# A decoder layer on one core: the order of its first phase rewritten, with 64-row self scores and both normalisations on ScalarE

## The chip, the cores and the metric

One core of a Trainium2 chip runs the whole kernel in one launch. The metric is the device time of an execution in microseconds (us); lower is better.

## What is computed

A transformer decoder layer (post-norm) over x of shape (32, 64, 256) with a context of the same shape:

```
h = LN(x + selfattn(x))              # 16 heads of 16, causal over 64 positions
h = LN(h + crossattn(h, ctx))        # 8 heads of 8 over the 256 channels as positions, rotary, softmax over 256
y = LN(h + ffn(h))                   # 256 -> 1024 -> 256, both matmuls with quantised weights and activations
def selfattn(x):  att = softmax(mask(q @ k.T / 4)); return (att @ v) @ w_out.T
def crossattn:    scores = rot(Wq x + bq) . rot(Wk c + bk) / sqrt(8); out = softmax(scores) @ (Wv c + bv); Wo out + bo
def ffn:          silu, gelu, LN, quantised linear layers
```

The self-attention has sequences of 64; the cross-attention treats the 64 positions of a sequence as channels and the 256 channels as its positions. Outer residuals and norms are those of the kernel's own stages (norm1, norm2, and the last norm in phase 3).

## The kernel before

The 32 sequences are taken as 16 pairs of 2 x 64 = 128 rows. Three phases follow each other, with a barrier between: the attention phase (the one that is changed), then two feed-forward phases, which take no part in the change but for norm2 of the last pair.

**Work of a pair in the attention phase.** Self-attention: qk_proj and v_proj (TensorE, fp32), qk_copy and v_copy (ScalarE), k_mask (GpSimd; the keys of a head are cut out by a mask so that one matmul gives several heads), scores (TensorE: a bf16 mask matmul, then fp32 scores on top in the same bank), minus_max (VectorE, row maxima, then the difference into SP), self_exp (ScalarE), self_sum (VectorE), self_norm (GpSimd), transpose_p, pt_copy, self_pv, ao_copy, out_proj. Then norm1_stats (VectorE), rstd (GpSimd), norm1 (VectorE, into X1), x_keep (ScalarE, X1 into XALL), rotary_proj q, rotate q (VectorE), split_parts q (GpSimd, three bf16 parts of an fp32 value), and over HBM into the expanded tile QA (store_parts, expand_rows). The context goes the same way to KA (rotary_proj k, rotate k, split_parts k). Cross-attention: sixteen tiles of max matmuls (mx_b) with a VectorE row maximum each; the maxima are negated in two bf16 parts (negate), transposed by TensorE (max_transpose), copied (mt_copy) and sent by two DMAs into rows 48 and 49 of QA (max_rows); sixteen tiles of exp matmuls (e_b) with ScalarE's exp into PB; eight pv_quad (P.V into u_b); u_copy, u_transpose, u_norm, att_transpose, at_copy, x_out_proj, norm2_stats, rstd, norm2 (VectorE), square_sum (ScalarE).

**Order.** It is written out by hand. Body i has sixteen steps S0 to S15, and all engines walk through them. In each step TensorE computes one max tile, 14 tiles ahead of the exp tiles (AHEAD), and one exp tile of pair i, two heads each, interleaved; every second step has a pv_quad. The other operations are put at fixed steps. A max tile needs the reduction of the tile two before it, an exp tile the exp of the one two before it. Everything else shares two PSUM banks, g_b[0] and g_b[1]: `use` makes TensorE wait, before it writes a bank, until the last reader of the group that was written there before is done, in the order of the program. So the order of the steps sets the waits.

Before, pair i+3 has its qk_proj at S0, v_proj at S11 and scores at S13 and S14 of body i, and its softmax, transposes, self_pv, out_proj, norm1 and q projection in S0 to S9 of body i+1. A prologue ahead of body 0 does three pairs by hand in three sets of banks (head_banks, tail_banks).

**Lines.** L443 qk_proj, L451 v_proj, L458 and L462 scores, L474 transpose_p, L487 self_pv, L496 out_proj, L508 and L509 rotary_proj, L516 xv_proj, L531 max tiles, L545 max_transpose, L559 exp tiles, L574 pv_quad, L230 u_transpose, L237 att_transpose, L242 x_out_proj; ScalarE L684 qk_copy, L702 self_exp, L709 pt_copy, L723 mt_copy, L729 exp_tile; GpSimd L818 k_mask, L823 self_norm, L831 to L841 split_parts; VectorE L850 and L854 minus_max, L862 and L864 self_sum, L869 to L873 norm1_stats, L880 norm1, L888 rotate, L278 to L283 norm2_stats, L287 norm2, L897 xv_bias, L907 max tiles, L918 and L920 negate.

## Time and profile before

| | |
|---|---|
| runs shown | 670.93 us median of 3 (668.68 to 674.22) |
| the profiled execution | 677.3 us, span 675.4 us from the first to the last instruction |
| TensorE, VectorE busy | 490.2 us (73%), 522.3 us (77%) |
| ScalarE, GpSimd busy | 378.3 us (56%), 319.9 us (47%) |
| mean granted clock of TensorE | 0.829 of full |
| DMA | 37.04 MB, mean 55 GB/s |

The attention phase takes the first 494 us of the span, the two feed-forward phases the rest. "Granted clock" is what the throttle leaves of TensorE's 2.4 GHz: 1.00 or 0.50. A stage is named by body: body i begins with the first exp tile of pair i.

### The profile page before, as it was taken

Reading aid. Unit: us, or ns where it says so; the run is one execution under the profiler, and the core shown is the slowest. Engines: PE = TensorE matmul, PEld = TensorE weight load, DVE = VectorE, ACT = ScalarE, POOL = GpSimd, SP = SyncE. Lnnn points to the kernel's source line nnn. Section 1 sums busy time; section 2 is a strip of 40 time slices with the busy share of each in tenths; the row PEclk is TensorE's granted clock in tenths of the full one; section 3 lists DMA queues with packets and bytes.
Section 4 is the critical chain, followed back from the end, with each engine's and each line's share of the span. In section 5 each row is a group of like instructions: output and inputs, shape, how many; then the busy total and the mean of one; then the engine's idle time right before and its main releaser. Section 6 shows DMA issues by size and latency. Waiting matters only on the chain. (4 is left out here: it accounts for less than half of the span.)

```text
span 675.4 us, 12183 instructions
## 1 busy us (share of the span) xinstructions
PE 490.2 (73%) x3986; PEld 253.3 (38%) x4002; DVE 522.3 (77%) x1045; ACT 378.3 (56%) x681; POOL 319.9 (47%) x383
## 2 busy tenths in 40 slices
PE   5556888889888888898898888788966414545445
PEld 3332435444444344444443444333222103333333
DVE  6476678978988879889888898778437677888885
ACT  1211346555556555555565656477548958677673
POOL 6442435364464553644645537320020057776773
PEclk9787779999999999999999999878567955555555
DMA  7212522212222223132222221220000000000000
GB/s 260 59 43 74 177 67 65 68 51 74 75 65 62 64 68 83 49 76 69 72 60 66 66 77 49 51 71 4 1 0 1 0 0 8 16 16 23 16 17 32
DMA packets 51400, 37.04 MB, mean 55 GB/s; under 512 B 21392, under 2 KB 47376, under 8 KB 51216
## 3 DMA queue, kind: packets, MB, share of 16 engines
q1 hardware_dynamic: 51344, 36.33, 18.8%
q8 instruction: 31, 0.51, 0.3%
q14 instruction: 25, 0.20, 0.1%
HBM read 24.52 MB, written 10.49 MB: 52 GB/s over the span
## 5 line engine op out<-in xcount | busy, mean ns | idle before, releaser
L729 ACT ACTIVATE PB<-e_b 128x512 f32<-128x512 f32 x256 | 149.5, 594 | 115.7 <-PE e_b L559 115.3
L907 DVE TENSOR_REDUCE MX<-mx_b 128x2 f32<-128x512 f32 x256 | 171.4, 681 | 44.0 <-PE mx_b L531 43.2
L531 PE MATMUL mx_b<-KA,QA 48*128 48x256 bf16 x512 | 101.3, 287 | 15.0 <-DMA QA<-parts_q 8.4
L559 PE MATMUL e_b<-QA,KA 50*128 50x256 bf16 x512 | 99.5, 289 | 9.6 <-DMA QA<-MR 7.4
L574 PE MATMUL u_b<-PB,VA 128*32 128x256 f32 x1024 | 88.7, 420 | 4.2 <-ACT PB L729 4.1
L823 POOL TENSOR_TENSOR SP<-SP,srec 128x1024 f32<-128x1024 f32 x14 | 26.6, 1901 | 101.4 <-DVE srec L864 101.4
L531 PEld LDWEIGHTS mx_b<-KA,QA 48*128 48x128 bf16 x512 | 31.5, 96 | 96.3 <-DVE MX L907 41.9
L1325 PE MATMUL r_b<-att_tab,Q 128*128 128x128 f32 x128 | 31.5, 427 | 37.5 <-ACT Q L1249 37.4
L818 POOL TENSOR_TENSOR KM<-QK,att_tab 128x1024 f32<-128x1024 f32 x30 | 57.0, 1904 | 1.6 <-ACT QK L684 1.6
L1317 PE MATMUL z_b<-w2q,Q2T 128*128 128x256 bf16 x128 | 30.2, 417 | 37.0 <-ACT Q2T L1272 26.3
L295 POOL TENSOR_TENSOR rs<-mv,epsc 128x1 f32<-128x1 f32 x32 | 6.1, 190 | 96.2 <-DVE mv L283 66.6
L1282 POOL TENSOR_TENSOR rsh<-mvh,epsc 128x1 f32<-128x1 f32 x16 | 15.2, 949 | 56.9 <-DVE mvh L1345 56.9
L1325 PEld LDWEIGHTS r_b<-att_tab,Q 128*128 128x128 f32 x128 | 25.1, 223 | 45.2 <-ACT Q L1249 38.1
L1292 POOL TENSOR_TENSOR N<-N,row_tab 128x1024 f32<-128x1024 f32 x16 | 37.6, 2349 | 1.9 <-ACT N L1256 1.9
L559 PEld LDWEIGHTS e_b<-QA,KA 50*128 50x128 bf16 x512 | 30.0, 96 | 20.1 <-DMA QA<-MR 11.1
L574 PEld LDWEIGHTS u_b<-PB,VA 128*32 128x32 f32 x1024 | 21.2, 112 | 40.4 <-ACT PB L729 25.6
L443 PE MATMUL g_b<-XT,wp 128*128 128x128 f32 x224 | 32.1, 303 | 5.7 <-DMA XT<-in_xT 5.7
L1317 PEld LDWEIGHTS z_b<-w2q,Q2T 128*128 128x128 bf16 x128 | 16.6, 141 | 49.3 <-DVE stz L1363 24.9
L443 PEld LDWEIGHTS g_b<-XT,wp 128*128 128x128 f32 x224 | 29.3, 211 | 11.0 <-DMA wp<-in_wpT 5.7
L462 PE MATMUL g_b<-KM,QK 128*64 128x512 f32 x112 | 30.2, 618 | 3.3 <-issue 3.3
L880 DVE TENSOR_SCALAR X<-Y,mv,rs 128x256 f32<-128x256 f32 x16 | 27.3, 1707 | 5.4 <-POOL rs L297 5.4
L831 POOL TENSOR_TENSOR full_k<-rot_k 128x256 f32<-128x256 f32 x16 | 11.6, 726 | 39.6 <-DVE rot_k L888 39.6
(197 smaller groups left out, 1125.4 us busy)
## 6 DMA issues: line engine op xcount, KB each, us to landing
KA<-parts_k SPq DMA_DIRECT2D x64, 96.0 KB
QA<-parts_q SPq DMA_DIRECT2D x64, 96.0 KB
parts_q<-part_q SPq DMA_DIRECT2D x32, 128.0 KB, 1.9
parts_k<-part_k SPq DMA_DIRECT2D x16, 192.0 KB, 2.1
XT<-in_xT SPq DMA_DIRECT2D x16, 128.0 KB, 2.4
X<-in_x SPq DMA_DIRECT2D x16, 128.0 KB, 2.2
C<-in_ctx SPq DMA_DIRECT2D x16, 128.0 KB, 2.1
out_y<-O SPq DMA_DIRECT2D x16, 128.0 KB, 1.7
```

Of the source, the lines that this page charges most:

```text
L443: last = nc.tensor.matmul(ps[:, P * c:P * c + P], wp[:, k, P * c:P * c + P], XT[:, a.p, k, :], start=k == 0, stop=k == 1)
L462: last = nc.tensor.matmul(ps[SEQ * b:SEQ * b + SEQ, :], QK[:, c, SEQ * b:SEQ * b + SEQ], KM[:, c, :, SEQ * b:SEQ * b + SEQ], start=False, ...
L531: m = nc.tensor.matmul(mx_b[n % 2][:, D * k:D * k + D], QA[low:low + K_MAX, 2 * i.ring + b, h, P * u:P * u + P], KA[low:low + K_MAX, 2 * i ...
L559: m = nc.tensor.matmul(e_b[n % 2][:, D * k:D * k + D], KA[low:low + K_EXP, 2 * i.ring + b, h, P * sc:P * sc + P], QA[low:low + K_EXP, 2 * ...
L574: last = nc.tensor.matmul(u_b[b][32 * j:32 * j + 32, D * s4:D * s4 + D], VA[:, i.p, sc, b, 4 * s4 + j, :], PB[:, (2 * m + j % 2) % 4, j // ...
L729: nc.scalar.activation(PB[:, n % 4].rearrange("p e t -> p (e t)"), e_b[n % 2][:, :], ACT.Exp, scale=XC ** -0.5).then_inc(e_sb.sem, 1)
L818: ops.tensor_tensor(KM[:, c], QK[:, 2 + c, :].unsqueeze(1).broadcast_to([P, 8, P]), kmask.unsqueeze(2).broadcast_to([P, 8, P]), ALU.mult). ...
L880: nc.vector.tensor_scalar(X1[:], Y1[:], mv1[:, 0:1], rs1[:, 1:2], ALU.subtract, ALU.mult).then_inc(ln1.sem, 1)
L907: nc.vector.tensor_reduce(MX[:, b, e, 2 * q:2 * q + 2, u], mx_b[n % 2][:, :].rearrange("p (e s) -> p e s", e=2), AXL.X, ALU.max).then_inc( ...
L1292: nc.gpsimd.tensor_tensor(N[:, k.p, :], N[:, k.p, :], gam, ALU.mult).then_inc(zg.sem, 1)
L1317: m = nc.tensor.matmul(z_b[j.p][:, 0:D], Q2T[:, j.p, k, :], w2q[:, k, :], start=k == 0, stop=k == 7)
L1325: t = nc.tensor.transpose(r_b[j.p][:, P * k:P * k + P], Q2[:, j.p, P * k:P * k + P], ident)
```

## The change

Only the attention phase is changed (and norm2 of the last pair). 

- Order: the whole self-attention of pair i+3 up to self_pv lies in body i (qk_proj S1, scores S5, transpose_p S13, self_pv S14); out_proj, norm1 and the q projection follow in S0 to S3 of body i+1. The prologue is gone: the bodies run from -4 (LEAD) and leave out what isn't there yet. All of it uses g_b[0] and g_b[1].
- Scores: k_mask makes 4 heads per chunk instead of 8; after two mask matmuls there are eight score matmuls of 64 rows, 64 columns and 256 moving columns, row half r into bank g_b[r], with one signal at the end. The row maximum and the difference go bank by bank, at S5 to S8; the exp is in two halves.
- Maxima of the cross-attention: MX (fp32) goes through TensorE as an fp32 matmul against the identity; mt_copy writes the negated high part (bf16) and mt_low (VectorE) the low part, instead of the two negations ahead of the transposition. The two DMAs of max_rows carry high and low rows instead of the two halves.
- norm1 and norm2 are applied by ScalarE (scale and bias), straight into XALL; rstd (GpSimd) gets a third operation for the bias. norm2_max stays on VectorE.
- The bias of the cross values is added after the softmax, in at_copy; xv_bias (VectorE) becomes xv_copy (ScalarE).
- Start: the fill of KA moves from GpSimd to VectorE, the small fills, VM and VA to GpSimd; the context has four buffers; row_tab is loaded later. TensorE waits for the two casts before its first matmul.
- SP's order per body: expand k, max_rows(i,1), store and expand q, loads, max_rows(i+1,0), store k, cross_values.

```diff
-            def scores(a, chunks=(0, 1)):
-                for c in chunks:
-                    ps = use(head_banks(a)[1 - c], sc_sub, a, 2 * c + 2)
+            def scores(a):
+                for r in range(2):
+                    ps = use(g_b[r], sc_sub, a, 2 * r + 2)
                     nc.tensor.matmul(ps[:, :], identb[:], maskb[:].rearrange("p h s -> p (h s)"),
                                      start=True, stop=False, skip_group_check=True)
+                for c in range(2):
                     wait(pe, km, a, c + 1)
-                    for b in range(2):
-                        last = nc.tensor.matmul(ps[SEQ * b:SEQ * b + SEQ, :], QK[:, c, SEQ * b:SEQ * b + SEQ],
-                                                KM[:, c, :, SEQ * b:SEQ * b + SEQ],
-                                                start=False, stop=True, skip_group_check=True)
-                    last.then_inc(sc_ps.sem, 1)
+                    for r in range(2):
+                        for b in range(2):
+                            last = nc.tensor.matmul(g_b[r][SEQ * b:SEQ * b + SEQ, D * c:D * c + D],
+                                                    QK[HALF * r:HALF * r + HALF, c, SEQ * b:SEQ * b + SEQ],
+                                                    KM[HALF * r:HALF * r + HALF, c, :, SEQ * b:SEQ * b + SEQ],
+                                                    start=False, stop=True, skip_group_check=True)
+                last.then_inc(sc_ps.sem, 1)
...
             def max_transpose(i, b, g):
-                ps = use(g_b[g], mt_sb, i, b + 1)
-                wait(pe, negm, i, 2 * b + 2)
-                nc.tensor.transpose(ps[0:32, 0:64].bitcast(BF16), NM[:].rearrange("p e m c -> p (e m c)"),
-                                    identb[:]).then_inc(mt_ps.sem, 1)
+                ps = use(g_b[g], mt_sb, i, 2 * b + 2)
+                wait(pe, mx_red, i, 8 * b + 8)
+                nc.tensor.matmul(ps[0:16, 0:P], MX[:, b].rearrange("p e h u -> p (e h u)"), ident,
+                                 start=True, stop=True).then_inc(mt_ps.sem, 1)
...
-            pe.wait_ge(ld_wp, 16)
-            qk_proj(p0)
-            v_proj(p0)
+            pe.wait_ge(ld_wp, 16)
             pe.wait_ge(s_tab, 2)
...
 TensorE, body(i), a = i+3, j = i+2, after the two pairs of matmuls of step s:
+                    if s == 0 and real(prev):   pv_quad(prev, 7)
+                    if s == 0 and real(j):      out_proj(j)
+                    if s == 1 and real(a):      qk_proj(a)
+                    if s == 2 and real(prev):   u_transpose(pe, prev, 1, use(g_b[0], u_nrm, prev, 4))
+                    if s == 2 and real(i):      max_transpose(i, 1, 1)
+                    if s == 3 and real(j):      rotary_proj("q", g_b[0], j)
+                    if s == 4 and real(prev):   att_transpose(pe, prev, use(g_b[1], at_sb, prev, 1))
+                    if s == 5 and real(a):      scores(a)
+                    if s == 7 and real(prev):   x_out_proj(pe, prev, use(g_b[0], ln2, prev, 1))
+                    if s == 10 and real(nxt):   max_transpose(nxt, 0, 1)
+                    if s == 10 and real(a):     rotary_proj("k", g_b[0], a)
+                    if s == 12 and real(i):     u_transpose(pe, i, 0, use(g_b[0], u_nrm, i, 2))
+                    if s == 12 and real(nxt):   xv_proj(nxt)
+                    if s == 13 and real(a):     transpose_p(a)
+                    if s == 14 and real(a):     self_pv(a)
+                    if s == 15 and real(i.plus(4)): v_proj(i.plus(4))
+                    if s and s % 2 == 0 and real(i): pv_quad(i, s // 2 - 1)
...
 VectorE, body(i), after the max tile of step s:
+   0: norm1_stats(j)   2: u_norm(prev, 1)   3: mt_low(i, 1), rotate q(j)   5, 7: row_max(a, r)
+   6, 8: minus_max(a, r)   9: norm2_stats(prev)   10: self_sum(a)   11: mt_low(nxt, 0), rotate k(a)
+   12: u_norm(i, 0)   14: norm2_max(prev)
 ScalarE, body(i), after the exp tile of step s:
+   0: u_copy(prev, 1)   1: qk_copy(a)   2: mt_copy(i, 1), norm1(j)   4: at_copy(prev)   7, 9: self_exp(a, r)
+   10: u_copy(i, 0), mt_copy(nxt, 0)   11: norm2(prev)   12: xv_copy(nxt)   13: pt_copy(a)
+   14: ao_copy(a), square_sum(prev)   15: v_copy(i+4)
 GpSimd, body(i):
+   rstd(ln1, j), k_mask(a), split q(j), rstd(ln2, prev), self_norm(a), split k(a)
...
-            for t, v in ((ones, 1.0), (halves, -0.5), (rnd, ROUND), (nrnd, -ROUND), (epsc, EPS), (half, -0.5)):
-                nc.vector.memset(t[:], v).then_inc(s_init, 1)
-            nc.vector.memset(VM[:], 0.0).then_inc(s_init, 1)
+            for e in range(2):
+                nc.vector.memset(KA[HALF * e + 32:HALF * e + 64].rearrange("p a h t -> p (a h t)"), 1.0).then_inc(s_pad, 1)
...
+            def norm1(a):
+                wait(act, ln1, a, 6)
+                nc.scalar.activation(XALL[:, a.v, :], Y1[:], ACT.Identity, bias=rs1[:, 2:3], scale=rs1[:, 1:2]).then_inc(ln1.sem, 1)
...
+            def mt_low(i, b, g):
+                wait(dve, mt_sb, i, 2 * b + 1)
+                nc.vector.scalar_tensor_tensor(out=MR[32:48, :], in0=g_b[g][0:16, 0:P], scalar=-1.0, in1=MR[0:16, :],
+                                               op0=ALU.mult, op1=ALU.subtract).then_inc(mt_sb.sem, 1)
```

The order of the bodies is condensed here to one line per operation; the calls are those of the changed kernel.

## Rows read from the trace of the kernel before

**Rows 1.** Windows by body: us, busy and count per engine, clock, DMA, GB/s.
```profile
71.60:102.00 30.40, 26.64 (x223) 14.35 (x225) 20.64 (x38) 14.06 (x28) 13.19 (x15) 0.83 0.38 125
102.00:426.70 324.70, 278.67 (x2718) 141.67 (x2733) 276.61 (x529) 184.21 (x386) 168.91 (x204) 1.00 0.25 66
426.70:453.70 27.00, 22.43 (x200) 10.45 (x196) 19.80 (x42) 16.52 (x32) 10.37 (x15) 0.82 0.20 53
453.70:494.10 40.40, 33.97 (x255) 11.33 (x255) 23.43 (x48) 25.83 (x48) 1.48 (x4) 0.66 0.03 10
```

**Rows 2.** Timeline of TensorE, body 6: start, us, line, tiles, count, idle before.
```profile
243.34 0.23 PE L545 MATMUL g_b<-identb,NM 128*32 128x128 bf16 x1
...
244.37 1.06 PE L474 MATMUL g_b<-att_tab,SP 128*128 128x128 f32 x8 [0.47 <-ACT MR L723]
245.36 0.64 PE L574 MATMUL u_b<-PB,VA 128*32 128x256 f32 x8
245.93 0.28 PE L531 MATMUL mx_b<-KA,QA 48*128 48x256 bf16 x1
...
246.25 0.69 PE L487 MATMUL g_b<-PT,VM 128*32 128x64 f32 x32
...
249.92 0.70 PE L242 MATMUL g_b<-AT,xw_all 128*128 128x256 f32 x2
...
252.76 0.70 PE L508 MATMUL g_b<-X,xw_all 128*128 128x256 f32 x2 [1.25 <-DVE X L880]
...
253.82 0.28 PE L531 MATMUL mx_b<-KA,QA 48*128 48x256 bf16 x1
...
260.83 0.39 PE L458 MATMUL g_b<-maskb,identb 128*128 128x512 bf16 x1
261.15 1.08 PE L462 MATMUL g_b<-KM,QK 128*64 128x512 f32 x4
262.16 0.64 PE L574 MATMUL u_b<-PB,VA 128*32 128x256 f32 x8
```

**Rows 3.** Groups of VectorE in bodies 1 to 12: count, busy us, mean ns, idle before.
```profile
L907 DVE TENSOR_REDUCE MX<-mx_b 128x2 f32<-128x512 f32 x193 | 129.6, 681 | 24.7 <-PE mx_b L531 24.5
L880 DVE TENSOR_SCALAR X<-Y,mv,rs 128x256 f32<-128x256 f32 x12 | 23.7, 1976 | 2.9 <-POOL rs L297 2.9
...
L862 DVE TENSOR_REDUCE ssum<-SP 128x16 f32<-128x1024 f32 x12 | 14.6, 1218 | 0.0
...
L888 DVE SCALAR_TENSOR_TENSOR rot_k<-g_b,xb_all,rot_tab 128x256 f32<-128x256 f32 x24 | 10.4, 474 | 0.4 <-PE g_b L509 0.3
...
L278 DVE SCALAR_TENSOR_TENSOR Y<-g_b,xb_all,XALL 128x256 f32<-128x256 f32 x12 | 5.6, 468 | 0.0
...
L281 DVE BATCH_NORM_STATS2 st<-Y 128x6 f32<-128x256 f32 x12 | 5.1, 428 | 0.4
```

**Rows 4.** Groups of all engines over the whole span: k_mask and the copies of transpose_p.
```profile
L818 POOL TENSOR_TENSOR KM<-QK,att_tab 128x1024 f32<-128x1024 f32 x30 | 57.0, 1904 | 1.6 <-ACT QK L684 1.6
...
L709 ACT ACTIVATE PT<-g_b 128x512 f32<-128x512 f32 x30 | 16.4, 595 | 11.4 <-PE g_b L474 11.4
```

**Rows 5.** Windows around two stretches at the low clock, columns as in rows 1.
```profile
426.70:430.10 3.40, 1.46 (x16) 0.56 (x12) 3.33 (x5) 1.66 (x4) 1.33 (x1) 1.00 0.41 117
430.10:433.50 3.40, 3.11 (x16) 1.50 (x16) 2.29 (x7) 0.60 (x1) 0.56 (x1) 0.50 0.10 10
...
88.80:95.60 6.80, 6.80 (x39) 3.54 (x37) 3.63 (x9) 2.79 (x7) 3.40 (x5) 0.50 0.28 86
```

**Rows 6.** Timeline of TensorE at 430 us, columns as in rows 2.
```profile
430.39 0.39 PE L531 MATMUL mx_b<-KA,QA 48*128 48x256 bf16 x1 [1.74 <-DMA QA<-parts_q]
```

**Rows 7.** Timeline of VectorE ahead of body 0: a fill, norm1 of pairs 0 and 1.
```profile
20.44 1.76 DVE L951 MEMSET VA<- 128x2048 f32 x1 [0.38 <-issue]
...
32.67 0.42 DVE L869 TENSOR_TENSOR Y<-g_b,X 128x256 f32<-128x256 f32 x1 [6.55 <-PE g_b L496]
...
53.49 0.42 DVE L869 TENSOR_TENSOR Y<-e_b,X 128x256 f32<-128x256 f32 x1 [6.22 <-PE e_b L496]
```

More of the change, by code:

```diff
@@ L297, in rstd @@
             nc.gpsimd.tensor_tensor(rs[:, 1:2], rs[:, 0:1], half[:], ALU.pow).then_inc(ev.sem, 1)
+            wait(pool, ev, i, 5)
+            nc.gpsimd.tensor_scalar(rs[:, 2:3], mv[:, 0:1], rs[:, 1:2], -1.0, ALU.mult, ALU.mult).then_inc(ev.sem, 1)
         def bodies(eng, body):
-            for k in range(NPAIR):
-                body(Pair(0, k), first=k == 0, selfs=k < 13, rotary=k < 14, last=k == 15)
+            for k in range(-LEAD, NPAIR):
+                body(Pair(0, k))
         @block.sync
@@ L427, in _ @@
+            bodies(sp, body)
         @block.tensor
@@ L594, in _ @@
-            rotary_proj("k", mx_b[1], p1)
-            qk_proj(p1)
-            v_proj(p1)
-            transpose_p(p0)
-            self_pv(p0)
-            out_proj(p0)
-            scores(p1)
-            rotary_proj("q", g_b[1], p0)
-            qk_proj(p2)
-            v_proj(p2)
-            xv_proj(p0)
-            transpose_p(p1)
-            self_pv(p1)
-            out_proj(p1)
-            scores(p2)
-            rotary_proj("q", e_b[1], p1)
-            wait(pe, ro_sb["k"], p1, 2)
-            for n in range(8):
-                max_tile(p0, n)
@@ L644, in body @@
-                    if s == 4 and rotary:
-                        transpose_p(j)
-                    if s == 5 and rotary:
-                        self_pv(j)
-                    if s == 6 and rotary:
-                        out_proj(j)
-                    if s == 6 and not first:
+                    if s == 2 and real(prev):
+                        u_transpose(pe, prev, 1, use(g_b[0], u_nrm, prev, 4))
+                    if s == 2 and real(i):
+                        max_transpose(i, 1, 1)
@@ L671, in body @@
+                    if s == 13 and real(a):
+                        transpose_p(a)
+                    if s == 13 and i.v == 13:
+                        weight_total(1)
+                    if s == 14 and real(a):
+                        self_pv(a)
+                    if s == 15 and real(i.plus(4)):
+                        v_proj(i.plus(4))
+                    if s and s % 2 == 0 and real(i):
                         pv_quad(i, s // 2 - 1)
@@ new lines, in body @@
+            def body(i):
+                prev, nxt, j, a = i.plus(-1), i.plus(1), i.plus(2), i.plus(3)
+                for s in range(16):
+                    ahead, n = tile_at(i, s + AHEAD)
+                    if real(ahead):
+                        max_tile(ahead, n)
+                    if s == 0 and real(j):
+                        norm1_stats(j)
+                    if s == 2 and real(prev):
+                        u_norm(dve, prev, 1, 0)
+                    if s == 3 and real(i):
+                        mt_low(i, 1, 1)
+                    if s == 3 and real(j):
+                        rotate("q", g_b[0], j)
+                    if s in (5, 7) and real(a):
+                        row_max(a, (s - 5) // 2)
+                    if s in (6, 8) and real(a):
+                        minus_max(a, (s - 6) // 2)
+                    if s == 9 and real(prev):
+                        norm2_stats(dve, prev, 0)
+                    if s == 10 and real(a):
+                        self_sum(a)
+                    if s == 11 and real(nxt):
+                        mt_low(nxt, 0, 1)
+                    if s == 11 and real(a):
+                        rotate("k", g_b[0], a)
+                    if s == 12 and real(i):
+                        u_norm(dve, i, 0, 0)
+                    if s == 14 and real(prev):
+                        norm2_max(dve, prev)
+                    if s == 14 and i.v == 13:
@@ L1110, in body @@
                 if at(i, 4):
-                    norm2(dve, pair)
+                    norm2_max(dve, pair)
                 if on[0]:
@@ L1176, in body @@
                 if at(i, 4):
+                    norm2(act, pair)
                     square_sum(act, pair)
```

541 lines of the change are left out of this document (214 added, 327 removed).

## The prediction

> **What bounds the kernel now.** I read the windows by stage first. Until the first exp tile 71.6 us pass; body 0 takes 30.4 us; bodies 1 to 12 take 324.7 us, 27.06 each; body 13 takes 27.0; bodies 14 and 15 take 40.4 [rows 1]. The two feed-forward phases behind them (181 us) don't change. So twelve equal bodies decide. In them TensorE is busy 278.7 of 324.7 us, 23.2 per body, and VectorE 276.6, 23.05 per body; ScalarE (15.4) and GpSimd (14.1) have room. Neither of the two is full alone: they hand PSUM banks to each other in order. The timeline of one body shows how [rows 2]: TensorE packs its groups without a gap and stops only where a bank or an operand is late. The largest stop, 1.25 us, is for norm1, and the groups say why: that 128x256 pass takes VectorE 1.98 us [rows 3].
>
> **What goes.** From VectorE's queue go norm1, the apply pass of norm2, the bias pass on the cross values, and the negations; a 16-row pass (mt_low, bound 0.2 to 0.5 us, taken 0.3) comes twice. On ScalarE norm1 costs nothing new (it takes x_keep's place); norm2 and xv_copy are short passes in an engine that is half idle, and the exp of SP in halves is covered likewise. GpSimd's k_mask halves (2 x 1.9 us [rows 4], to about 2 x 1.1) and pays for the third operation of rstd. The 1.25 us stop goes: out_proj now stands at S0, and norm1 (statistics 1.1, rstd about 1.2, ScalarE 0.4) has the 4.4 us of TensorE work up to S3; it arrives about 0.2 us early. What is late next, if it isn't, is rotary q itself. The stops for DMAs go too: q is rotated at S3 instead of S9. On SP's queue max_rows(i+1,0) now stands behind both expansions and the loads, about 13 us of issues in a body of 27, and is needed only at the next S0: covered.
>
> **TensorE's work.** Scores: before, per half one mask matmul and two 128-row matmuls side by side; the four records take 1.01 us to the next group [rows 2], with the mask 1.33, so 2.65 per pair. After: two masks (0.55) and eight matmuls of 64x64 over 256 columns. Max and exp matmuls, 48 and 50 rows at different partitions, run side by side in these records (the pair of tiles takes 0.32 us to the next group [rows 2]), so four quarters at once are likely: half the columns, twice the sharing, 1.0 us. If none ran side by side beyond two: 2.0. I take 1.55 in all, a saving of 1.1. The fp32 max transpose costs about 0.1 more. TensorE's work: 23.2 - 1.1 + 0.1 = 22.2 us a body.
>
> **The new order, walked once.** I follow both queues from the end of the score matmuls in S5. VectorE then holds, in this order: row_max 0, max tile, minus_max 0, max tile, row_max 1, max tile, minus_max 1, max tile (eight 128x512 passes; 0.68 each by the mean, in a full queue some 0.63 apart, since the groups of these bodies add up to more than the busy time: 5.0), norm2_stats (0.47 + 0.43 + about 0.2: 1.05), max tile (0.63), self_sum with its reciprocal (1.22 + about 0.25), max tile (0.63), mt_low (0.3), rotate k (two of 0.47) [rows 3]: **10.0 us**, with no gap, because scores end with a single signal and nothing of it can start before. In that time TensorE has seven pairs of tiles (0.32), three P.V quads (0.57), x_out_proj (0.70 less the overlap of 0.07 that all records show: 0.63), rotary k (1.06) and a max transpose (0.23 in bf16, taken 0.25) [rows 2]: 5.9 us. It stops at x_out_proj (the bank is freed by minus_max 0), at the max transpose (needs tile 7 of the next pair reduced), and above all at u_transpose in S12, whose bank is freed only by rotate k: from the pass that frees the bank for rotary k (L278) TensorE has 2.3 us to do and VectorE 4.5, so **2.2 us idle in one piece**. From there to the next score end TensorE leads: 22.2 - 5.9 = 16.3 us, plus 0.5 where self_pv follows transpose_p with only a pair of tiles between (the transposes take 1.0, their two copies of 0.6 [rows 4] end 1.8 after the start): 16.8. Body: 10.0 + 16.8 = **26.8 us** against 27.06, 3 us less over twelve. I keep 0.6 us a body either way for passes that overlap more or less than this. What the change takes from VectorE it mostly takes where TensorE leads, and it gathers the score passes, self_sum and rotate k where VectorE leads.
>
> **The clock.** In bodies 1 to 12 the granted clock stays at full (1.00, 2.4 GHz) [rows 1] with stops of up to 1.25 us. Ahead of 430 us TensorE is busy 1.46 of 3.4 us, with one stop of 1.74 us [rows 5, 6], and the stretch behind shows 0.50 (1.2 GHz) for 3.4 us; before 95.6 us it is low for 6.8 us though TensorE is busy throughout [rows 5]. The new order has 4.1 us idle in each 10, 2.2 in one piece, in every body. I expect a fall in each, landing in the part where TensorE leads. Price: body 0 ran with a mean clock of 0.83, which is 10.3 us at the low level, and was 3.35 us longer than its followers [rows 1]: 0.33 us lost per us; where nothing hides it 0.5. With 3.4 to 6.8 us low per body, 5.1 x 0.4 = 2.0 us (bounds 1.1 and 3.4). Body: **28.8 us**, 12 x 1.75 = +21 us.
> The Trainium skill ("TensorE: Matmul & The Clock Gate", section on HAM oscillation) speaks against this: the gaps that it warns of are longer than any here. By it the clock would hold and the sum would be the first rival's. The stop at 430 us is nearer to the case than the page, so I follow the row.
>
> **Head.** The KA fill moves to VectorE, ahead of the casts for which TensorE now waits: 2 x 6144 elements a partition at 0.86 ns (1.76 us for 2048 [rows 7]) are 10.6 us, so TensorE starts at about 12.0 instead of 5.7. Bounds: half that per bf16 element (start at 7), or as taken. The skill ("VectorE: DVE Perf Modes", on zero memsets) has one cycle per element whatever the type; at its 0.96 GHz that is 12.8 us, a start 2 us later. Then pair 0's chain: 27 us from TensorE's start to the first norm1 pass before (32.67), about the same after (38); from there to pair 1's 20.8 before [rows 7], 22 after, since GpSimd's rstd now precedes the mask and the q split precedes the norm. The hand-made overlap of three pairs in different banks is gone. From pair 1's pass (60) to the first exp tile body -1 needs qk_proj, rotary q and scores (8), VectorE's stretch without norm2 (8.9) and S12 to S15 (5): 82 against 71.6, **+10.5** (bounds +3 and +14). Body 0 mostly at the low clock as before: 29.5, -0.9.
>
> **Tail.** Body 13 loses all of pair 15's self-attention behind the scores, which now lies in body 12. What is left is bodies 14 and 15 (20.2 each [rows 1]) plus out_proj, norm1 and rotary q: 21.5, **-5.5**.
>
> **Sum.** Profiled execution: 677.3 + 10.5 - 0.9 + 21 - 5.5 = 702.4. The median of the runs shown is 670.93, 0.9906 of the profiled one: **696 us**.
>
> **Rivals.**
> 1. The clock holds. Bodies of 26.8: -3 over twelve, body 0 -3.6, head +10.5, tail -5.5: 675.7, which is 669. For it: the stops in the equal bodies were survived, and the skill's page. Against: 430 us. Chance 0.22.
> 2. Faster: VectorE's stretch is shorter than ten us, because its passes start earlier than the score signal lets me think, or overlap more. TensorE's own work is only 22.2, so every 0.1 us counts 1.3 us over bodies 0 to 12, and with less idle time the clock holds. It turns into a gain over 1% once a body takes under 26.4; with a stretch of 8 us bodies of 24.8 give 677.3 - 27 - 5.6 + 10.5 - 5.5 = 650, on the median's footing 643. Against: the passes are all measured and stand in one in-order queue. Chance 0.18.
> 3. The change doesn't do what it says: the quarters of the score matmuls don't run four at once. +1.0 us a body on top of the forecast: 715, which is 709. Chance 0.10.
> My forecast has 0.50. 1% (6.7 us) is about what a measurement of this kernel can tell from no change. My forecast and rival 3 are slower by more, but for 0.05; rival 1 (669, give or take 8) splits into 0.06 faster, 0.12 same, 0.04 slower; rival 2 is faster. Together: faster 0.25, same 0.17, slower 0.58. The range: up, 3.4 us of clock a body and a head of +14 make 716; down, rival 1 with an early head gives 658; what lies beyond is most of rival 2.
>
> **What the next profile would show.** VectorE full from the end of the score matmuls to rotate k, 9.5 to 10.5 us; TensorE's longest stop before L230 behind rotate k, about 2 us, twelve times and more; no stop before rotary q; the granted clock of the middle windows well under 1.00; the first exp tile near 82 us; a short body 13. Wrong I would be first by the clock: if it reads 1.00 throughout, the answer is rival 1. Next by the head: if VectorE's fill of KA is quick, 5 us of the loss go.

## The result and the profile after

The changed kernel takes **689.94 us** (median of 4 runs, 688.72 to 690.93), the kernel before 671.39 on the same chip; ratio 1.0275, 95% interval 1.0228 to 1.0322. It is slower, by 18.6 us. Its profiled execution took 690.93, its span 689.3. That of the kernel before took 677.3, well above its own median, so the two traces lie only 13.9 us apart.

Windows of the changed kernel by body, cut at the first exp tile of each (columns as in rows 1): body 0, bodies 1 to 12, body 13, bodies 14 and 15, and two pieces of body 5.

```profile
89.50:118.70 29.20, 24.64 (x230) 12.54 (x230) 18.18 (x34) 15.05 (x30) 11.78 (x16) 0.85 0.44 135
118.70:446.30 327.60, 272.16 (x2834) 145.80 (x2844) 235.59 (x468) 198.12 (x418) 152.83 (x228) 0.97 0.24 65
446.30:468.00 21.70, 17.76 (x158) 7.69 (x158) 15.41 (x34) 15.90 (x32) 5.42 (x11) 0.89 0.17 51
468.00:508.50 40.50, 34.25 (x258) 13.29 (x258) 22.39 (x42) 27.06 (x51) 2.89 (x6) 0.68 0.01 2
244.80:248.20 3.40, 1.45 (x18) 0.47 (x16) 3.30 (x7) 1.57 (x3) 2.40 (x4) 1.00 0.61 180
248.20:251.60 3.40, 3.22 (x20) 2.01 (x20) 1.28 (x4) 0.38 (x1) 3.16 (x6) 0.51 0.08 23
```

Against [rows 1] the span changes in four places: the head is 17.9 us longer (89.5 instead of 71.6), body 0 1.2 shorter, bodies 1 to 12 together 2.9 longer (327.6 instead of 324.7), body 13 5.3 shorter. The twelve bodies tell most. VectorE's busy time in them fell from 276.6 to 235.6 us and TensorE's from 278.7 to 272.2, and yet they are no shorter. By the starts of their first exp tiles six of bodies 1 to 11 take 26.80 us each, and bodies 1, 2, 5, 8 and 11 take 28.22 to 28.31. Each of these five holds one stretch of 3.4 us in which the granted clock is 0.50, TensorE's 1.2 GHz. The last two rows show one, in body 5: 3.4 us at the full clock in which TensorE is busy 1.45 us, with the stop of 2.14 us for u_transpose at their end, then 3.4 us at half.

TensorE's timeline in body 6 (columns as in rows 2):

```profile
265.40 0.38 PE L448 MATMUL g_b<-maskb,identb 128*128 128x512 bf16 x1 [0.16 <-issue]
265.71 1.09 PE L454 MATMUL g_b<-KM,QK 64*64 64x256 f32 x16
266.74 0.28 PE L525 MATMUL mx_b<-KA,QA 48*128 48x256 bf16 x1
...
268.81 0.70 PE L245 MATMUL g_b<-AT,xw_all 128*128 128x256 f32 x2 [0.79 <-DVE SP L820]
...
271.91 0.38 PE L539 MATMUL g_b<-att_tab,MX 128*16 128x128 f32 x2 [0.89 <-DVE MX L859]
...
276.65 0.65 PE L233 MATMUL g_b<-att_tab,US 128*128 128x128 f32 x4 [2.14 <-DVE rot_k L850]
...
280.46 0.65 PE L480 MATMUL g_b<-PT,VM 128*32 128x64 f32 x30 [0.46 <-ACT PT L671]
```

VectorE's timeline in the same body, its first pass on the scores and the two of rotate k:

```profile
266.87 0.69 DVE L812 TENSOR_REDUCE smax<-g_b 128x8 f32<-128x512 f32 x1 [0.91 <-PE g_b L454]
...
275.72 0.88 DVE L850 SCALAR_TENSOR_TENSOR rot_k<-g_b,xb_all,rot_tab 128x256 f32<-128x256 f32 x2
```

And what TensorE waited for in bodies 1 to 12 (us in total, times, longest):

```profile
PE g_b L233 <- DVE rot_k L850: 25.7, 12, 2.1
PE g_b L539 <- DVE MX L859: 10.7, 12, 0.9
PE g_b L245 <- DVE SP L820: 9.5, 12, 0.8
PE g_b L480 <- ACT PT L671: 5.5, 12, 0.5
```

The 1.25 us stop for norm1 [rows 2] is gone. In its place stand three stops for VectorE in one stretch: 0.79, 0.89 and, for the bank that rotate k frees, 2.14 us. From the first row maximum to the end of rotate k (266.87 to 276.60) VectorE works without a gap. The eight quarter-size score matmuls take 1.03 us (265.71 to 266.74); four at a time were forecast to take 1.0 and two at a time 2.0, so they do run four at once.

The head, VectorE first (a memset of 6144 bf16 elements, the cast that TensorE waits for, the residual sums of pairs 0 and 1), then TensorE's first group:

```profile
2.07 5.18 DVE L885 MEMSET KA<- 32x6144 bf16 x1 [2.07 <-issue]
8.59 5.18 DVE L885 MEMSET KA<- 32x6144 bf16 x1 [1.34 <-issue]
...
13.94 0.42 DVE L888 CAST maskb<-att_tab 128x512 bf16<-128x512 f32 x1
...
41.36 0.42 DVE L838 TENSOR_TENSOR Y<-g_b,X 128x256 f32<-128x256 f32 x1 [9.53 <-PE g_b L489]
...
64.22 0.42 DVE L838 TENSOR_TENSOR Y<-g_b,X 128x256 f32<-128x256 f32 x1 [9.41 <-PE g_b L489]
```

```profile
14.46 2.04 PE L441 MATMUL g_b<-wp,XT 128*128 128x256 f32 x4 [14.46 <-DVE maskb L888]
```

That group takes 1.13 us in a body. The clock is low over 17.1, 10.2 and 17.1 us (from 26.4, 53.7 and 74.2), which is 42.7 of the 89.5 us of the head. The head of the kernel before was low as well, for 30.6 of its 71.6 us (from 23.9, 44.4 and 61.5).

### The profile page after: what moved, and what is told of

Its sections match the earlier page's. It is cut to its first block and busy times, and to the rows that moved or that the text cites. A ratio compares the mean times of both kernels' runs of the same rounds, so it can differ in the third digit from the quotient of the medians.

```text
span 689.3 us, 12444 instructions
## 1 busy us (share of the span) xinstructions
PE 483.6 (70%) x4146; PEld 262.7 (38%) x4162; DVE 465.4 (68%) x950; ACT 398.5 (58%) x729; POOL 302.5 (44%) x430
## 5 line engine op out<-in xcount | busy, mean ns | idle before, releaser
L859 DVE TENSOR_REDUCE MX<-mx_b 128x2 f32<-128x512 f32 x256 | 173.5, 682 | 88.2 <-PE mx_b L525 86.6
L568 PE MATMUL u_b<-PB,VA 128*32 128x256 f32 x1024 | 93.1, 422 | 4.8 <-ACT PB L692 4.7
L1225 PE MATMUL z_b<-w2q,Q2T 128*128 128x256 bf16 x128 | 29.4, 409 | 36.8 <-ACT Q2T L1180 26.1
L781 POOL TENSOR_TENSOR KM<-QK,att_tab 128x512 f32<-128x512 f32 x32 | 32.6, 1040 | 29.5 <-ACT QK L646 29.4
L233 PE MATMUL g_b<-att_tab,US 128*128 128x128 f32 x128 | 24.1, 318 | 28.6 <-DVE rot_k L850 27.4
L786 POOL TENSOR_TENSOR SP<-SP,srec 128x1024 f32<-128x1024 f32 x16 | 30.4, 1901 | 28.9 <-DVE srec L831 28.9
L812 DVE TENSOR_REDUCE smax<-g_b 128x8 f32<-128x512 f32 x32 | 22.0, 686 | 25.7 <-PE g_b L454 25.7
L432 PE MATMUL g_b<-XT,wp 128*128 128x128 f32 x256 | 35.5, 296 | 2.3 <-ACT VM L657 2.3
L568 PEld LDWEIGHTS u_b<-PB,VA 128*32 128x32 f32 x1024 | 25.2, 112 | 27.9 <-issue 17.6
L432 PEld LDWEIGHTS g_b<-XT,wp 128*128 128x128 f32 x256 | 33.0, 207 | 6.0 <-ACT VM L657 3.0
L441 PE MATMUL g_b<-wp,XT 128*128 128x256 f32 x64 | 21.8, 471 | 15.7 <-DVE maskb L888 14.5
```

The costliest lines, as they stand in the source:

```text
L432: last = nc.tensor.matmul(ps[:, P * c:P * c + P], wp[:, k, P * c:P * c + P], XT[:, a.p, k, :], start=k == 0, stop=k == 1)
L568: last = nc.tensor.matmul(u_b[b][32 * j:32 * j + 32, D * s4:D * s4 + D], VA[:, i.p, sc, b, 4 * s4 + j, :], PB[:, (2 * m + j % 2) % 4, j // ...
L781: nc.gpsimd.tensor_tensor(KM[:, c], QK[:, 2 + c, :].unsqueeze(1).broadcast_to([P, 4, P]), kmask.unsqueeze(2).broadcast_to([P, 4, P]), ALU. ...
L786: ops.tensor_tensor(SP[:], SP[:], srec[:].unsqueeze(2).broadcast_to([P, SH, SEQ]), ALU.mult).then_inc(s_norm.sem, 1)
L859: nc.vector.tensor_reduce(MX[:, b, e, 2 * q:2 * q + 2, u], mx_b[n % 2][:, :].rearrange("p (e s) -> p e s", e=2), AXL.X, ALU.max).then_inc( ...
L1225: m = nc.tensor.matmul(z_b[j.p][:, 0:D], Q2T[:, j.p, k, :], w2q[:, k, :], start=k == 0, stop=k == 7)
```

## Experiments

Each ratio is to the kernel before, run beside the edited one (670.0 to 671.8 us). The edits are condensed; `...` marks what is left out. A trace is of one execution, and two executions can differ in how long the clock is low where the edit changes nothing: the head of experiment 2 ends 1.8 us earlier than that of the changed kernel, although its edit starts in body 0.

Theory at the outset: the loss is (a) memsets ahead of the casts, (b) the low clock in the head, (c) the 2.1 us stop, by its length and by the falls of the clock behind it; and what the change gains, it gains with norm1. Rival: the parts are worth about nothing one by one, and the body is set by something the order doesn't touch.

**1. Casts first.** The changed kernel with
```
+dve.wait_ge(ld_att, 16)
+nc.vector.tensor_copy(identb[:], ...); nc.vector.tensor_copy(maskb[:], ...)
 for e in range(2): nc.vector.memset(KA[...], 1.0)
-dve.wait_ge(ld_att, 16)
-nc.vector.tensor_copy(identb[:], ...); nc.vector.tensor_copy(maskb[:], ...)
```


> The changed kernel with one edit: VectorE makes the two casts first and fills KA after them. Theory (late start): in the changed kernel TensorE's first matmul comes at 14.4 us, after the second cast, and the fills of 5.18 us each stand ahead of it; with the casts first the start is about 7 us earlier, everything behind moves by the same amount, the first exp tile comes at 82 to 83 us instead of 89.5, and the kernel takes about 683 us instead of 690. The fills then end near 18 us and nobody needs them before the first expansion near 40 us. Rival (the chain is held elsewhere): the start is held by the weights' landing or ScalarE's table load, and the first exp tile moves by less than 2 us: 688 to 690.

680.83 us, ratio to before 1.0131 (1.0052 to 1.0210). TensorE starts at 6.36 instead of 14.46, the first exp tile at 80.9 instead of 89.5; bodies as in the changed kernel (26.80, and 28.2 about every third). With the memsets behind the casts 8.6 of the 17.9 us of the head are gone, 8.1 of them by the earlier start. A little of the memsets' cost is left: pair 0's first row maximum starts at 19.31, right behind the second memset (14.10 to 19.28), and 1.3 us after its scores.

**2. TensorE kept busy in the long stop.** Seven matmuls that nobody reads, ahead of u_transpose:
```
+if s == 12 and real(i) and real(a):
+    pe.wait_ge(e_sb.sem, 16 * i.v + 12)
+    for _ in range(7): nc.tensor.matmul(e_b[1][:, :], identb[:], maskb[...], start=True, stop=True)
```


> The changed kernel plus seven matmuls (128x128 by 512 columns, bf16, 0.21 us each) that nobody reads, written in S12 into the exp bank that is free, ahead of u_transpose, in bodies 0 to 12. They fill 1.5 of the 2.14 us for which TensorE stands idle there. Theory (the stop in S12 makes the clock fall): the granted clock stays at 1.00 from body 1 to body 12, every one of these bodies takes 26.8 us, where five of them took 28.3, and the kernel is 7 to 9 us faster, about 682. Rival (the falls have another cause): the low stretches of 3.4 us stay, and the time is the same or, if the matmuls get in the way, up to 0.3 us a body longer: 690 to 694.

681.87 us, ratio 1.0168 (1.0115 to 1.0220). A window of this kernel over most of the twelve bodies:
```profile
110.00:440.00 330.00, 294.82 (x3042) 153.64 (x3038) 241.13 (x478) 204.34 (x431) 155.53 (x233) 1.00 0.25 70
```
The clock stays at 1.00, and bodies 1 to 11 take 26.80 us each: the 1.4 to 1.5 us that five of them had on top was the clock's. So the falls cost 7.3 us in those bodies, and with the stop filled they don't come: in this kernel the clock fell on that stop.

**3. The long stop removed by order.** u_transpose(i, 0) ahead of rotary k, VectorE's passes to match:
```
-if s == 10: rotary_proj("k", g_b[0], a)          # TensorE
-if s == 12: u_transpose(pe, i, 0, ...)
+if s == 10: u_transpose(pe, i, 0, ...)
+if s == 12: rotary_proj("k", g_b[0], a)
-s == 10: self_sum(a);  s == 11: mt_low(nxt, 0, 1); rotate("k");  s == 12: u_norm(dve, i, 0, 0)   # VectorE
+s == 10: mt_low(nxt, 0, 1); u_norm(dve, i, 0, 0); self_sum(a);   s == 12: rotate("k")
```
(u_copy(i, 0) on ScalarE moves from S10 to S9 with it.)


> The changed kernel with the order of the middle period altered: the transposition of the normalised key/value rows of pair 0 one step earlier (S10), ahead of the rotary projection of k, which goes to S12; VectorE makes the low maxima and the normalised rows first and the rotation of k last. Nothing else is changed. Theory A (the 2.1 us stop of TensorE in front of the transposition is both the lost time of a body and what the clock falls on): the stop disappears, a body is about 25.6 us instead of 26.8, no stretch at the low clock between bodies 1 and 12 (5 of them at 1.47 us in the changed kernel): 690 less 13 x 1.15 less 7 is about 668. Theory B (VectorE's chain sets the body, and TensorE only waits for it somewhere else): a stop of 1 to 2 us shows at the transposition of the probabilities or at the rotary projections, the body stays at 26.8 us and the clock falls as before: 690.

670.12 us, ratio 0.9978 (0.9935 to 1.0021): level with the kernel before. From body 3 to body 11 the clock stays full and a body takes 26.02 us, where 25.6 was expected. What TensorE waits for in bodies 2 to 11 of this kernel:
```profile
PE g_b L539 <- DVE MX L859: 8.9, 10, 0.9
PE g_b L467 <- POOL SP L786: 8.9, 10, 1.0
PE g_b L245 <- DVE SP L820: 7.9, 10, 0.8
PE g_b L480 <- ACT PT L671: 4.6, 10, 0.5
PE g_b L233 <- ACT US L701: 2.6, 10, 0.3
```
Both theories had a part of it: of the 2.14 us stop 0.8 are gained, and 0.87 (in most bodies) come back as a stop at the transposition of the probabilities, since GpSimd's normalisation now starts later. But no stop is over 1 us, and the clock doesn't fall. Some 3.6 of the 19.8 us gained lie in the head, whose first exp tile comes at 85.9; its last low stretch lasts 6.8 us instead of 17.1, and whether the order or the execution did that isn't shown.

**4. TensorE kept busy in the head.** 93 unread matmuls in bodies -3 to -1, spread where it stands still:
```
+WARM = {-3: {1: 9, 5: 4, 10: 6, 13: 14, 14: 3, 15: 2}, -2: {3: 4, 5: 3, ...}, -1: {...}}
 for s in range(16):
+    for _ in range(WARM.get(i.v, {}).get(s, 0)):
+        nc.tensor.matmul(u_b[0][:, :], identb[:], maskb[...], start=True, stop=True)
```


> The changed kernel plus matmuls that nobody reads (128x128 by 512 columns, bf16) in bodies -3 to -1, into a u bank that is free until body 0, ahead of the groups for which TensorE waits: 38, 34 and 21 of them. Theory (the low clock makes the head longer): TensorE's groups in the chain run at 2.4 GHz (v_proj 1.13 instead of 2.07, qk_proj 2.05 instead of 3.79, transpose_p 1.1 instead of 1.97, out_proj 1.13 instead of 2.2), and the first exp tile comes 8 to 12 us earlier, near 79 us; the kernel takes 678 to 682 us. Rival (the head is held by the chain over the other engines, whatever the clock): 1 to 3 us at most, 687 to 689; matmuls that overrun a wait could cost up to 3 us.

680.93 us, ratio 1.0162 (1.0105 to 1.0219). First exp tile at 80.0, 9.5 earlier; of the head's low stretches one of 3.4 us is left. So in this head the low clock costs as much as the memsets do, though the two overlap: the next experiment but one has both. But this is not a loss against the kernel before by itself: that kernel's head runs at the low clock for 30.6 us too, only 12.1 less. The 17.9 us of the head aren't the sum of the two repairs, and what it costs by itself that the new head works on one pair at a time wasn't measured.

**5. norm1 back on VectorE in the changed kernel**, at S2:
```
-norm1(i.plus(2))                                  # ScalarE, S2
+nc.vector.tensor_scalar(XALL[:, j.v, :], Y1[:], mv1[:, 0:1], rs1[:, 1:2], ALU.subtract, ALU.mult)
```


> The changed kernel with the first normalisation alone put back on VectorE (one pass of 0.4 us, or 1.98 us where GpSimd holds it up, as in the kernel before), everything else of the change kept. Theory A (it is the normalisation on ScalarE that pays for the rest of the change, since VectorE leads in the first part of a body): the pass is held up by the 1.04 us mask products of GpSimd and lies in VectorE's chain, a body is 27.8 us instead of 26.8, the time 700 to 704. Theory B (the new order has slack for it, since TensorE leads the body): the body stays at 26.8 us, the time within 3 of 690.

692.25 us, ratio 1.0296 (1.0217 to 1.0376), no different from the changed kernel within the intervals; bodies of 26.67 without a fall. Theory A falls: in the new order norm1 on ScalarE is worth nothing that can be measured. The group of this kernel's VectorE over 110 to 400 us says why, and below it are one such pass and the two mask products that GpSimd makes meanwhile, of 1.04 us each:
```profile
L900 DVE TENSOR_SCALAR XALL<-Y,mv,rs 128x256 f32<-128x256 f32 x11 | 4.9, 450 | 0.0
...
124.28 0.45 DVE L900 TENSOR_SCALAR XALL<-Y,mv,rs 128x256 f32<-128x256 f32 x1
...
123.54 2.09 POOL L779 TENSOR_TENSOR KM<-QK,att_tab 128x512 f32<-128x512 f32 x2 [0.62 <-ACT QK L646]
```
At this place the same pass takes 0.45 us, not 1.98 [rows 3], in a part where TensorE leads. It starts only 0.3 us before the first product ends; for the first three pairs, where it starts within 0.3 us of the first product's start, it takes 1.25, 0.93 and 0.94 us.

**6. Experiments 1, 3 and 4 together.** Expected:


> The changed kernel with three edits together: the casts ahead of the memsets in the head, unread matmuls in the head that keep TensorE busy, and the other order in S10 and S12. If the three costs are separate: the head with both edits 11 to 12 us earlier (alone they gave 8.6 and 9.5 and share the low clock of the head), 13 bodies at 25.6 instead of 26.8 and no falls of the clock (22): 690 less 34 is about 656. If the order in S12 brings nothing: 690 less 12 is 678.

660.41 us, ratio 0.9856 (0.9779 to 0.9933): the changed kernel with these three repairs beats the kernel before by 10 us. That is 4 short of what was expected, mostly by the bodies, which were taken at 25.6. Bodies of 26.02, first exp tile at 75.8, 13.7 earlier than in the changed kernel and still 4.2 later than before, although the clock is now low for 10.2 us of the head, against 30.6 before.

**7. norm1 on ScalarE alone, on the kernel before.** Nothing else of the change:
```
-nc.vector.tensor_scalar(X1[:], Y1[:], mv1[:, 0:1], rs1[:, 1:2], ALU.subtract, ALU.mult)
-nc.scalar.activation(XALL[...], X1[:].unsqueeze(1), ACT.Copy)
+nc.gpsimd.tensor_scalar(rs[:, 2:3], mv[:, 0:1], rs[:, 1:2], -1.0, ALU.mult, ALU.mult)
+nc.scalar.activation(XALL[:, a.v, :], Y1[:], ACT.Identity, bias=rs1[:, 2:3], scale=rs1[:, 1:2])
```


> The kernel before with one part of the change alone: norm1 is applied by ScalarE straight into XALL (x_keep and X1 are gone), with the third operation of rstd. Theory (the pass on VectorE of 1.98 us was the cause of TensorE's longest stop): the stop of 1.25 us ahead of rotary q is gone and a body takes 25.7 to 25.9 us instead of 27.06; with 14 bodies the kernel takes 653 to 657 us instead of 671. Rival (another wait takes its place, as the bank freed by rotate q or DMA landings): the stop moves to the next group and a body takes 26.6 to 27.1: 665 to 672.

647.32 us, ratio 0.9653 (0.9583 to 0.9723), more than expected. Bodies 1 to 12 take 25.0 us on average (24.84 where nothing is late) instead of 27.06. The window of bodies 1 to 12 of this kernel, and its largest waits of TensorE there:
```profile
99.20:399.20 300.00, 280.16 (x2738) 141.73 (x2736) 255.83 (x517) 186.59 (x386) 171.54 (x216) 1.00 0.26 72
```
```profile
PE u_b L576 <- ACT PB L731: 4.3, 9, 0.5
PE g_b L510 <- ACT XALL L744: 4.0, 12, 0.7
PE g_b L476 <- ACT MR L725: 4.0, 11, 0.5
...
PE mx_b L533 <- DMA QA<-parts_q: 0.8, 3, 0.3
```
TensorE is busy 93% of the time, with no stop over 1 us: this is what the body looks like when TensorE sets it. With the stop for norm1 the waits for the DMAs shrink too: to 1.3 us for the row maxima and 0.8 for the parts of q, from 6.4 and 6.7. So one part of the change alone, in the old order, is worth 23 us; all the rest, added to it, costs 43 (689.9 less 647.3). The parts don't add up: in the new order the same part is worth nothing (experiment 5).

**8. The 64-row scores on top of 7**, order and maxima as before:
```
-for c in chunks: mask; 4 matmuls of 128 rows x 512 columns per pair
+for r in range(2): mask;  for c, r, b: matmul(banks[r][64b:64b+64, 256c:...], QK[64r:..., c, ...], KM[64r:..., c, ...])
```


> The kernel before with the first normalisation on ScalarE (which alone gave 647.3 and bodies of 24.84 us) and with the 64-row self scores, eight matmuls instead of the four on 128 rows; order, maxima and the second normalisation as in the kernel before. Theory A (TensorE now leads a body, and the 64-row scores take 1.1 us for eight instead of 2.65): a body 0.5 to 1.1 us shorter and the time 633 to 641. Theory B (VectorE leads here too, TensorE waits for it elsewhere): the body stays at 24.8 us and the time at 647; the extra exponentials or a mask product could even make it longer.

648.54 us, ratio 0.9645 (0.9566 to 0.9725). The scores are as short as in the changed kernel, here in one body:
```profile
242.20 1.09 PE L466 MATMUL g_b<-KM,QK 64*64 64x256 f32 x16
```
but the 1.1 us come back as waits (bodies 1 to 11, us in total, times, longest):
```profile
PE mx_b L536 <- DVE MX L906: 12.9, 19, 0.9
PE mx_b L536 <- DMA QA<-parts_q: 4.8, 7, 2.0
```
Theory B: TensorE reaches the next max tile earlier and waits for VectorE, which has the same passes as before. Bodies 1 to 11 take 25.0 us on average here and in experiment 7. A saving on TensorE where VectorE is next in line was worth nothing. In this kernel the clock falls once, from 372.1 to 375.5, though no stop in the ten us ahead of it is over 0.94 us:
```profile
369.59 0.28 PE L536 MATMUL mx_b<-KA,QA 48*128 48x256 bf16 x1 [0.92 <-DVE MX L906]
370.81 0.28 PE L564 MATMUL e_b<-QA,KA 50*128 50x256 bf16 x1 [0.94 <-DMA QA<-MR]
...
372.10:375.50 3.40, 3.40 (x19) 2.87 (x18) 1.35 (x2) 1.15 (x3) 1.90 (x1) 0.50 0.51 112
```

**9. Why norm1 took 1.98 us.** The trace of the kernel before has, at one such pass, GpSimd's second mask product and norm1:
```profile
250.66 1.89 POOL L818 TENSOR_TENSOR KM<-QK,att_tab 128x1024 f32<-128x1024 f32 x1
250.72 1.98 DVE L880 TENSOR_SCALAR X<-Y,mv,rs 128x256 f32<-128x256 f32 x1 [0.23 <-POOL rs L297]
```
I tried another form of instruction first, at the same place:
```
-nc.vector.tensor_scalar(X1[:], Y1[:], mv1[:, 0:1], rs1[:, 1:2], ALU.subtract, ALU.mult)
+nc.vector.scalar_tensor_tensor(out=X1[:], in0=Y1[:], scalar=mv1[:, 0:1],
+                               in1=rs1[:, 1:2].broadcast_to([P, D]), op0=ALU.subtract, op1=ALU.mult)
```


> The kernel before with one instruction changed: the first normalisation stays on VectorE at its place, but as a scalar_tensor_tensor (rows less the mean, times the reciprocal deviation read as a second tensor operand) instead of a tensor_scalar. Theory A (the 1.98 us of the tensor_scalar is GpSimd's mask product holding it up, since in all 12 bodies it ends with that product, and the same form takes 0.40 us where GpSimd is still; the other form, 0.47 us for the rotations that lie beside GpSimd's work, is not held): the pass takes 0.47 us, a body is 1.5 us shorter or a little more, 13 bodies give 20 us or more: 646 to 654. Theory B (the pass is slow for another reason, or only its removal from VectorE pays): it stays near 2 us and the time at 670.

673.78 us, ratio 1.0062 (1.0019 to 1.0105): no gain. Its tile X in this kernel (min/median/max of 16, ns):
```profile
L880 DVE SCALAR_TENSOR_TENSOR X<-Y,mv,rs x16: 485/2108/2110, 34.7 to 441.9; 128x256 f32<-128x256 f32 x16
```
0.49 us where no product runs beside it, 2.11 where one does. Theory A's premise on the form was wrong: the rotations read one operand from PSUM and, looked at again, don't lie beside GpSimd's work in any body. TensorE's stop at rotary q, behind this pass, grew from 1.25 to 1.38 us and more, and behind three of the twelve the clock fell (in bodies 4, 10 and 11, at 195.9, 359.8 and 387.1); the first:
```profile
195.61 0.94 PE L508 MATMUL g_b<-X,xw_all 128*128 128x256 f32 x2 [1.38 <-DVE X L880]
...
195.90:199.30 3.40, 3.40 (x16) 1.92 (x19) 3.26 (x10) 1.67 (x4) 0.96 (x3) 0.50 0.19 65
```
Then the product was moved instead:
```
-if selfs: k_mask(pool, nc.gpsimd, a, (1,))
 if not first: rstd(pool, ln2, i.plus(-1), mv2, rs2)
+if selfs: k_mask(pool, nc.gpsimd, a, (1,))
```


> The kernel before with one thing moved: GpSimd's second mask product of 1.89 us, which starts just ahead of the first normalisation in every body, is issued behind the two small operations for the deviation of the second normalisation, some 3 us later. The normalisation stays on VectorE, in the same form at the same place. Theory A (VectorE's pass is held up for as long as that product runs, whatever form the pass has, since with another form it took 2.1 us too): the pass takes 0.40 us, TensorE's 1.25 us stop at the rotary projection of q goes, a body is 1.0 to 1.6 us shorter, 650 to 657; the product then lies beside the second statistics and the rotation of q, and the parts of q come up to 1.9 us later, which can take some of it back. Theory B (the pass itself takes 2 us at that place for another reason): it stays at 1.98 us and the time at 670.

663.32 us, ratio 0.9896 (0.9855 to 0.9936) against 671.75 beside it. In this kernel VectorE, then GpSimd, in body 6:
```profile
244.84 0.41 DVE L880 TENSOR_SCALAR X<-Y,mv,rs 128x256 f32<-128x256 f32 x1 [0.24 <-POOL rs L297]
```
```profile
247.27 0.55 POOL L297 TENSOR_TENSOR rs<-rs,half 128x1 f32<-128x1 f32 x1
247.78 1.90 POOL L818 TENSOR_TENSOR KM<-QK,att_tab 128x1024 f32<-128x1024 f32 x1
```
```profile
247.83 0.87 DVE L888 SCALAR_TENSOR_TENSOR rot_q<-g_b,xb_all,rot_tab 128x256 f32<-128x256 f32 x2
```
The pass takes 0.41 us, on VectorE, in its old form: it was the product that held it. The last row answers what the first form couldn't: the two rotations of q, with one operand from PSUM, now do lie beside the product, and they take no longer than before. Bodies are 26.1 us, 1.0 shorter, at the edge of what was expected, and the time stays 6 above it. Part of the gain is taken back: in bodies 1 to 12 TensorE now waits 14.3 us for the DMA of the row maxima, 6.4 before; why that DMA comes later wasn't looked into.
The Trainium skill ("SBUF — State Buffer", section "Who interferes with whom") says that a VectorE instruction in a two-port mode or with two inputs in SBUF, and a GpSimd one that reads SBUF, exclude each other for the whole of the one that came first. These three traces agree: 1.98 and 2.11 us beside the product, ending 0.15 and 0.28 us after it, and 0.41 away from it.

**10. The other pass that GpSimd holds**, the rounding of the maxima (0.17 us in half its calls, about 1.0 in the other), on top of 7, as a scalar_tensor_tensor; then that with 8.
```
-nc.vector.tensor_scalar(NM[:, :, 0, :], MX[:, b]..., -1.0, None, ALU.mult)
+nc.vector.scalar_tensor_tensor(out=NM[:, :, 0, :], in0=MX[:, b]..., scalar=-2.0, in1=MX[:, b]..., op0=ALU.mult, op1=ALU.add)
```


> The kernel before with the first normalisation on ScalarE (647.3, bodies of 24.84 us) and with the other tensor_scalar that GpSimd holds up, the rounding of the maxima to bf16 (0.17 us in one half of its calls and 0.95 to 1.05 in the other), as a scalar_tensor_tensor. Theory A (VectorE still leads the period it lies in): up to 0.8 us less in a body, 24.0 to 24.6, the time 637 to 644. Theory B (TensorE leads there): each call takes 0.17 us, the body stays at 24.8 and the time at 647.

> The edit of the last kernel together with the 64-row self scores (which alone gave 648.5 on the kernel with the normalisation on ScalarE, no gain over 647.3, bodies of 24.67 to 25.2 us). If VectorE's hold was what hid the shorter scores, both together give more than each alone: bodies of 23.7 to 24.2 us and 634 to 640. If the two do not meet, the time is that of the last kernel within 2.

646.88 us, ratio 0.9666 (0.9629 to 0.9703), and 648.30, ratio 0.9672 (0.9632 to 0.9713). Both are level with experiment 7 within the intervals. Neither theory's 0.17 us came: the group of the first of the two reads
```profile
L915 DVE SCALAR_TENSOR_TENSOR NM<-MX 128x16 bf16<-128x16 f32 x21 | 13.3, 634 | 0.7
```
as long as the tensor_scalar was in experiment 7 (635; 557 in the kernel before). The form again changes nothing, so these two say nothing on what a shorter pass would be worth; that stays open.

## Why the prediction came out as it did

The forecast was 696, slower by over 1%; the time is 689.9, slower by 2.8%. The mechanism of a body held, and two terms of the sum were off, in opposite directions: the clock term was 18.1 us too large and the head 7.4 too small. That they partly cancel is luck, and so is a part of how near 696 comes to 689.9 (see the footing).

**Right: the walk of one body.** VectorE's stretch was forecast at 10.0 us and took 9.7 (266.87 to 276.60), the stop behind rotate k at 2.2 and is 2.14, a body without the clock at 26.8 and takes 26.80. The stops at x_out_proj and at the max transpose are where they were put. Norm1 was to arrive 0.2 us early for rotary q, and TensorE waits 0.14 for it; mt_low is 0.28 (0.3), the mask products 2 x 1.04 (2 x 1.1), the scores with their mask matmuls 1.34 (1.55). That the body comes out so exactly is partly chance: VectorE's stretch is 0.3 shorter than forecast and the rest of the body 0.3 longer.

**Right: the tail.** Body 13 21.7 us (21.5), bodies 14 and 15 as before, body 0 29.2 (29.5).

**Mis-sized: the clock term**, +21 us with every body at 28.8. It was twelve falls of 5.1 us at 0.4 each, 24 us. Measured are five falls in twelve bodies, of 3.4 us each, which cost 1.47: 7.3 us, and +2.9 over the twelve bodies in place of +21. The price per us was right: 1.47 for 3.4 is 0.43, taken as 0.4. (The last 1.4 us are body 12, which takes 25.4.) The step that failed is "I expect a fall in each": one row at 430 us showed that a stretch with 1.46 us busy and a stop of 1.74 can be followed by a low one, and I made it a rule for a pattern that recurs. In the trace after, the stop of 2.14 us ahead of 248.2 has a fall behind it, while the same stop leaves the clock full in seven of twelve bodies. That the stop is the cause in this kernel is shown (experiments 2 and 3); which of the equal bodies it hits isn't settled by these runs. Nor is the length of one stop enough to tell: the clock fell behind one stop of 1.38 us in experiment 9 and behind two of 0.92 and 0.94 in experiment 8, and held behind 1.25 in eleven bodies of the kernel before. The rule of the Trainium skill ("TensorE: Matmul & The Clock Gate", HAM oscillation), by which the clock would hold, isn't borne out either: it fell behind a stop of 2.14 us, and with the stop filled it didn't.

Two readings of the trace before were off. The stops in the equal bodies go up to 1.43 us, not 1.25, and the clock held behind that one; and the low stretch at 88.8 us, "though TensorE is busy throughout", has a stop of 1.53 us for norm1 just ahead of it:
```profile
236.77 0.28 PE L559 MATMUL e_b<-QA,KA 50*128 50x256 bf16 x1 [1.43 <-DMA QA<-MR]
...
87.40 0.70 PE L508 MATMUL g_b<-X,xw_all 128*128 128x256 f32 x2 [1.53 <-DVE X L880]
```

**Mis-sized: the head**, +10.5 us, measured +17.9, beyond its upper bound of +14. TensorE starts at 14.46 instead of 12.0: the two memsets were right (5.18 each, 10.4 for my 10.6), but the first starts only at 2.07 and the second 1.34 us after the first ends. From there to pair 0's sum it is 26.9 us, to pair 1's 22.9, as forecast (26 and 22). From pair 1's sum to the first exp tile it is 25.3 instead of 22, at the low clock from 74.2 on. I had the low clock in the terms only as far as the old head had it, 30.6 us of it against 42.7 now; experiment 4 prices all of it at 9.5 us.

**The footing.** The sum for the profiled execution was 702.4 and its time 690.9; by the terms, 702.4 + 7.4 (head) - 18.1 (twelve bodies) - 0.3 (body 0) + 0.2 (body 13), less 0.5 in the phases behind, is 691.1. The profiled run of before was 0.9% above its median and that of after 0.1%, so that scaling brought the forecast 6.4 nearer to 690 than its terms were. The lower bound, 658, doesn't come out of its terms, which give 668.2 for the profiled execution and 662 for the median; nothing measured here hangs on it.

**The rivals.** Rival 1 (the clock holds, 669) was right on most bodies and too low by the head and by the scaling; experiment 2, the clock held but the head as it is, gives 681.9. The granted clock of the twelve bodies is 0.97, neither 1.00 throughout nor "well under". Rival 2 (a shorter stretch) and rival 3 (quarters not four at once) didn't occur. "What goes" named norm1's 1.98 us as the largest stop, and that is shown by experiment 7; what I didn't ask was why a pass of 256 elements takes 1.98 us when L278 with as many takes 0.47 [rows 3]. The answer (experiment 9) also says that most of the gain was to be had without the rest of the change.

## What to carry to other kernels

When a small pass is several times longer than its equals, find what runs beside it on the other engines before moving work; here one GpSimd product placed elsewhere, or the pass on ScalarE, gave 8 and 23 us, while the rest of the change cost 43. Before banks are handed round in a new order, add up what the slower engine holds between two handovers and what the other has to do meanwhile: that walk gave the body to 0.1 us. And price a new head by TensorE's clock as well as by its chain: both heads here ran at the low clock for over 40% of their time, and keeping TensorE busy in the new one gave 9.5 us.

The best version measured is the kernel before with norm1 on ScalarE, 647.3 us, 3.5% under the kernel before. The variants of experiments 8 and 10 on top of it are level with it.
